# An audio tower in one kernel: the setup joined to the first loop, with its arrays laid elsewhere and the scale of the first convolution made in four parts

## The reference

```python
# 1: first convolution, 9 taps, 64 -> 128 channels, 248 outputs a sequence
sq = sum(x * x, -1); wsq = windows of 9 of sq
wnorm = sqrt(max(wsq, 0))
scale = where(wnorm < 1, 1, 1 / (wnorm + 1e-7))      # one number a token
v = conv(x, kernel) * scale
h = relu(tanh(|v| * LAM) * sign(v) + bias)
# 2: state space layer on layernorm(h): projection to 644 columns,
#    4-tap convolution, silu, scan with decays (4 heads), gate, norm, projection
h = h + mamba2(layernorm(h))
# 3: 16 experts, 2 for each token, a shared layer, and a feed-forward layer
h = h + moe_and_ffn(layernorm(h))
```

## Time and profile before

| | |
|---|---|
| median of 3 runs | 1109.79 us (1109.08 to 1115.85) |
| the profiled execution | span 1108.8 us, time 1110.55 us |
| TensorE busy | 919.5 us (83%) |
| VectorE busy | 720.5 us (65%) |
| GpSimd busy | 588.3 us (53%) |
| ScalarE busy | 495.7 us (45%) |

### The profile page before, as it was taken

The page is one execution under the profiler, slowest core; times in us unless marked ns, Lnnn a source line. Parts: engine busy times, 40 slices in busy tenths (PEclk is TensorE's granted clock), DMA queues, the critical chain, the costliest instruction groups (busy, mean ns, idle before and its releaser), DMA issues. The chain is left out here.

```text
span 1108.8 us, 22495 instructions
## 1 busy us (share of the span) xinstructions
PE 919.5 (83%) x6227; PEld 769.8 (69%) x6228; DVE 720.5 (65%) x2073; ACT 495.7 (45%) x1212; POOL 588.3 (53%) x627
## 2 busy tenths in 40 slices
PE   0488999999999999999964049999999999398887
PEld 0367777778777777878753049999999989266665
DVE  4246887787888888788874225555555545488884
ACT  3243544544544454454423025555555545144443
POOL 3133554676777767667647505555555545233342
PEclk9889999999999999998986569999999999699999
DMA  6400000000000100000084112122222221223331
GB/s 134 104 10 10 10 11 11 29 20 29 16 24 29 30 26 22 20 15 15 19 253 144 52 51 68 54 59 63 60 62 67 62 58 48 74 56 92 92 91 37
DMA packets 72012, 58.97 MB, mean 53 GB/s; under 512 B 19136, under 2 KB 61435, under 8 KB 71952
## 3 DMA queue, kind: packets, MB, share of 16 engines
q1 hardware_dynamic: 63408, 41.88, 14.7%
q0 software_dynamic: 8544, 16.34, 4.5%
HBM read 35.62 MB, written 23.81 MB: 54 GB/s over the span
## 5 line engine op out<-in xcount | busy, mean ns | idle before, releaser
L1478 POOL DMA_INDIRECT y_tokens<-arena x139 | 157.3, 1132 | 162.1 <-DVE arena L1501 116.6
L1465 ACT ACTIVATE arena<-psum,arena 128x128 f32<-128x128 f32 x556 | 158.7, 369 | 135.0 <-PE psum L1439 125.2
L1439 PE MATMUL psum<-arena 128*128 128x128 f32 x1112 | 155.8, 284 | 7.3 <-issue 3.4
L1439 PEld LDWEIGHTS psum<-arena 128*128 128x128 f32 x1112 | 136.3, 193 | 19.6 <-issue 10.8
L1452 PE MATMUL psum<-arena 128*128 x1112 | 147.4, 275 | 0.4 <-ACT arena L1465 0.4
L1098 POOL DMA_INDIRECT x_slots<-arena,idx x128 | 127.5, 996 | 34.5 <-issue 34.5
L1493 DVE COPY arena<-arena 128x644 f32 x139 | 69.2, 498 | 110.4 <-issue 56.7
L1452 PEld LDWEIGHTS psum<-arena 128*128 128x128 f32 x1112 | 135.7, 192 | 0.6 <-issue 0.6
L1209 DVE TENSOR_TENSOR_SCAN arena<-psum,arena 124x496 f32<-124x496 f32 x64 | 72.6, 1175 | 18.3 <-PE psum L751 18.3
L1652 ACT ACTIVATE arena<-psum,b_f 128x496 f32<-128x496 f32 x64 | 43.1, 673 | 58.9 <-PE psum L1633 58.9
L1501 DVE TENSOR_TENSOR arena<-psum,arena 128x128 f32<-128x128 f32 x139 | 40.5, 292 | 39.3 <-PE psum L1452 18.4
(11 more groups left out here) (255 smaller groups left out, 2138.4 us busy)
## 6 DMA issues: line engine op xcount, KB each, us to landing
arena<-x_slots SPq DMA_DIRECT2D x139, 64.5 KB
arena<-y_tokens SPq DMA_DIRECT2D x16, 448.0 KB
arena<-in_x SPq DMA_DIRECT2D x16, 256.0 KB, 2.9
out_tokens<-arena SPq DMA_DIRECT2D x16, 224.0 KB
arena<-in_ew SPq DMA_DIRECT2D x1, 2304.0 KB
y_tokens<-arena POOLq DMA_INDIRECT x139
x_slots<-zero_src SPq DMA_DIRECT2D x33, 64.5 KB, 3.8
arena<-in_x SPq DMA_DIRECT2D x4, 512.0 KB, 6.8
```

Source lines behind the costliest of these rows:

```text
L1439: last = nc.tensor.matmul(psum[:, 2 + b.q % 2, k * 128:(k + 1) * 128], w1_blk[b.q % 4][:, k * 128:(k + 1) * 128], hT[b.q % 2], start=True, ...
L1465: last = nc.scalar.activation(EHT[t.q % 2][:, k * 128:(k + 1) * 128], psum[:, 2 + t.q % 2, k * 128:(k + 1) * 128], ACT.Silu, bias=w1_blk[t ...
L1478: nc.gpsimd.indirect_dma_start(out=y_tokens, out_offset=bass.IndirectOffsetOnAxis(ap=xb[t.q][:, F:F + 1].bitcast(i32), axis=0), in_=YO[t.q ...
```

## The change

1. **One block.** The setup's instructions move into the first loop's block, each into its engine's stream. The setup arrays no longer lie in the arena under the loop's arrays but in `h_all` (residual, from row block 24 on) and `moe_all` (mixture), which are first written in later steps. Offsets in the arena stay as they were.
2. **Loads in the order of use.** First unit 0, then `tokw`, the first quarter of all tokens, `w_in` and `cw` (own count `ld_proj`), the bias (`ld_bias`), the eight others of `ld_ssm`, unit 1, the other three quarters.
3. **Scale in four parts.** Part 0 is made in step 0 (its window sums stand inside `conv(0)`), part 1 in step 0 and 1, parts 2 and 3 in step 1 and 2 (`parts_at`). The root is now a power on GpSimd (`wnorm_of`). `tanh(a)` waits for its quarter.
4. **Activation table.** A one-element Silu is the first activation; the Sqrt on ScalarE is gone.
5. **Orders in the loop, for all steps.** VectorE: the short scans of the first half come after `x_rest` (`long_scans`, `short_scans`); `hn_rest` comes after `sum_squares` and the second part of `choose`. TensorE: `output(c)` comes before `hn_transposes(a)`, and the row sums (now `row_sums`) behind it.

```diff
@@ SP
                 load(0)
+                kw = tok_kernel.rearrange("k c f -> c k f")
+                sp.dma_start(tokw[0:64, 0:5, :], kw[:, 0:TAPS:2, :]).then_inc(ld_tok, 16)
+                sp.dma_start(tokw[64:128, 0:4, :], kw[:, 1:TAPS:2, :]).then_inc(ld_tok, 16)
+                all_tokens(0)
+                sp.dma_start(w_in, in_proj).then_inc(ld_proj, 16)
+                sp.dma_start(cw, rows(conv_w, 128)).then_inc(ld_proj, 16)
+                sp.dma_start(tokb[:, :], rows(tok_bias, CH)).then_inc(ld_bias, 16)
...
                 load(1)
+                for n in range(1, XPARTS):
+                    all_tokens(n)
@@
+        def part_of(n):
+            return slice(n * NCH // XPARTS, (n + 1) * NCH // XPARTS)
+        def parts_at(t):
+            return {0: [1], 1: [2, 3]}.get(t, [])
@@ TensorE
+                def windows(n):
+                    pe.wait_ge(row_squares_ready, n + 1)
+                    if n == 0:
+                        pe.wait_ge(bands_ready, 1)
+                    k = SEQS // XPARTS
+                    sqv = sq.rearrange("p (b j) -> p j b", j=2)[:, :, n * k:(n + 1) * k]
+                    for c in range(2):
+                        for j in range(2):
+                            last = nc.tensor.matmul(psum[0:CH, 7, 2 * n * k + c * k:2 * n * k + (c + 1) * k],
+                                                    band[:, 2 * j + c, :], sqv[:, j, :],
+                                                    start=(j == 0), stop=(j == 1))
+                    last.then_inc(windows_ready, 1)
...
                     for k in range(5):
+                        if a == 0 and k == 3:
+                            windows(0)
...
                     if a is not None: conv_rows(a)
+                    for n in parts_at(t): windows(n)
...
                     if d is not None: shared_down(d, a, b)
+                    if c is not None: output(c)
                     if a is not None: hn_transposes(a, d, t)
-                    if c is not None: output(c)
+                    if c is not None: row_sums(c)
@@ ScalarE
+                act.wait_ge(warm, 1)
+                nc.scalar.activation(warm_out[:, :], warm_in[:, :], ACT.Silu)
...
+                    if t == 0:
+                        act.wait_ge(tokw_padded, 1)
+                        act.wait_ge(ld_tok, 32)
+                        high_part(0)
...
                     if a is not None: x_copy(a)
+                    if t == 0:
+                        squares(0)
+                        act.wait_ge(ld_proj, 32)
+                        high_part(1)
+                        act.wait_ge(folded, 1)
+                        high_part(2)
...
                     if a is not None: tanh(a); relu(a)
+                    for n in parts_at(t): squares(n)
@@ GpSimd
+                def wnorm_of(n):
+                    pool.wait_ge(wsq_ready, n + 1)
+                    nc.gpsimd.tensor_tensor(wnorm[:, part_of(n)], wsq[:, part_of(n)],
+                                            half[0:CH, :].to_broadcast([CH, NCH // XPARTS]), ALU.pow)\
+                        .then_inc(wnorm_ready, 1)
+                wnorm_of(0)
+                pool.wait_ge(ld_ssm, 16 * 8)
...
                     if a is not None: rstd_of(a)
+                    for n in parts_at(t): wnorm_of(n)
@@ VectorE
+                low_part(0)
+                x_rest(0)
+                row_squares(0)
+                dve.wait_ge(ld_proj, 32)
+                cwv = cw.rearrange("p (c k) -> p k c", k=KC)
+                for k in range(KC):
+                    last = V.tensor_tensor(w_tap[:, k, :], w_in[:, DI:DI + 256], cwv[:, k, 0:256], ALU.mult)
+                last.then_inc(folded, 1)
+                window_squares(0)
+                low_part(1)
+                low_part(2)
+                scale_of(0)
...
-                    if c is not None: scans(c, 0)
+                    if c is not None: long_scans(c, 0)
                     if b is not None: dt_first(b)
-                    if a is not None: x_rest(a)
-                    if c is not None: decayed_scores(c, 0)
+                    if a: x_rest(a)
+                    if c is not None: short_scans(c, 0); decayed_scores(c, 0)
...
                     if a is not None: stats(a)
+                    for n in parts_at(t): row_squares(n); window_squares(n)
+                    for n in parts_at(t - 1): scale_of(n)
...
                     if d is not None: shared_out(d)
-                    if a is not None: hn_rest(a)
                     if c is not None: sum_squares(c)
                     for n in chosen(t): choose(n, ("second",))
+                    if a is not None: hn_rest(a)
                     if c is not None: mean_squares(c); residual(c)
```

More of the change, by code:

```diff
@@ L214, in take, with rows_for, part @@
             return v
+        def rows_for(home, first):
+            at = [first]
+            def part(parts, *shape):
+                n = 1
+                for k in shape:
+                    n *= k
+                v = home[0:parts, at[0]:at[0] + n]
+                at[0] += n
+                assert at[0] <= 8192, at[0]
+                if len(shape) == 2:
+                    v = v.rearrange("p (a b) -> p a b", b=shape[1])
+                return v
+            return part
         def take_pair(name, shape):
@@ L371, in audio_tower @@
         ld_tok = sem("ld_tok")
+        ld_bias = sem("ld_bias")
+        ld_proj = sem("ld_proj")
         ld_ssm = sem("ld_ssm")
@@ L1029, in _ @@
             def _(pool):
+                nc.gpsimd.memset(ident[:, :], 0.0)
+                nc.gpsimd.memset(half[:, :], 0.5)
+                link(pool, pool_step, nc.gpsimd.memset(band, 1.0))
+                nc.gpsimd.affine_select(out=ident[:, :], in_=ident[:, :], compare_op=ALU.not_equal, fill=1.0, base=0,
+                                        pattern=[[-1, 128]], channel_multiplier=1).then_inc(ident_ready, 1)
+                for j in range(2):
+                    for c in range(2):
+                        v = band[:, 2 * j + c, :]
+                        last = nc.gpsimd.affine_select(out=v, in_=v, compare_op=ALU.is_ge, fill=0.0,
+                                                       base=128 * j - CH * c, pattern=[[-1, CH]],
+                                                       channel_multiplier=1)
@@ new lines, in _ @@
+                link(pool, pool_step, last)
+                for j in range(2):
+                    for c in range(2):
+                        v = band[:, 2 * j + c, :]
+                        last = nc.gpsimd.affine_select(out=v, in_=v, compare_op=ALU.is_ge, fill=0.0,
+                                                       base=TAPS - 1 - 128 * j + CH * c,
+                                                       pattern=[[1, CH]], channel_multiplier=-1)
+                last.then_inc(bands_ready, 1)
@@ L1030, in _ @@
+                for j in range(3, -1, -1):
+                    last = nc.gpsimd.tensor_scalar(a_neg[:, j, :], a_neg[:, 0, :], -1.0, 0.0,
+                                                   ALU.mult, ALU.add)
+                link(pool, pool_step, last)
+                pool.wait_ge(ld_bias, 16)
                 last_slot = pool.to_reg(SLOTS - 1)
```

297 lines of the change are left out of this document (138 added, 159 removed).

## The result

| | median of all runs | runs | ratio, 95% interval |
|---|---|---|---|
| before | 1112.65 us (1109.08 to 1117.64) | 20 | |
| changed | 1108.81 us (1095.97 to 1115.65) | 20 | 0.9926 [0.9904, 0.9948] |
| the same once more, on another chip (e14 below) | 1101.16 us against 1108.83 | 11 and 16 | 0.9918 [0.9886, 0.995] |

The change is worth 0.7 to 0.8%, some 8 to 9 us, where 22.5 were forecast. The changed kernel also spreads over 20 us, the one before over 9. The first trace of it comes from the slowest of its 20 runs, 1115.65 us, which the ratio leaves out as slow, with three others that are over 1.5% above the fastest. The second comes from a run of 1093.02, near the fast end of e14. I show both, since they frame the kernel; neither is its median. The first `mean_squares` belongs to step 2, the last to step 17.

The account below looks back on a forecast made before the run. In the first loop's long middle TensorE's chain was taken as the bound (busy 442.88 of 480 us). Start 13.5 plus steps 9 gave 22.5 off 1109.79: 1087.3, called 1087; own range 1078 to 1098, over the cases 1070 to 1103.

Parts of the forecast that it names:

- the clock: Steps 3 to 15: splitting TensorE's long gap into 0.6 and 1.3 ends four half-clock stretches, gaining 6 us.
- the 0 for what lies behind the steady steps: Stages after the loop start from its end, their loads too, and move with it: 0 us.
- Step 0: Joined setup and first step: `stats(0)` starts at 23.0 us instead of 44.75, 21.7 earlier.
- the rival with the port in turn: Step 0: `low_part(1)`, GpSimd's power and `low_part(2)` run in a row; scale 2.0 us later, 1089 us; chance 0.08.
- Step 1 gives back: Step 1: window sums ahead of `projection(0,1)` on TensorE make `hn_transposes(1)` later, 8.8 us lost.
- Step 2: Step 2: `conv_rows(2)` gains 2.4 us from the clock; two scales before `skip_add(0,1)` cost 1.8 at `mean_squares(0)`.
- Start in all: Setup and steps 0 to 2 together: 13.5 us earlier, bounds 10 and 18.
- The short scans: Steps 3 to 15: moving them behind `x_rest` gains 0; TensorE waits 1.3 us more for cT at `conv_rows`.
- Row sums and `hn_rest`: Steps 3 to 15: the row sums' 0.4 us wait goes and `mean_squares` comes sooner in some steps; sum 3 us.
- another length there was named as a sign of being wrong: Stages after the loop: the forecast called itself wrong if they took another length.
- the 3 and the 6 of the sum: Steps 3 to 15: 3 us from row sums and `hn_rest`, 6 from the clock; sum 9, bounds 0 and 12.
- The slower rival: Clock drops behind the moved wait before `conv_rows` in each of 13 steps, costing 22 us: 1115 us; chance 0.06.

Follow-up runs that it names:

- e14: The changed kernel run once more unaltered, for a second trace, on another chip: ratio 0.9918 to the kernel before, 1101.16 us.
- e9: The changed kernel with 12 unused TensorE products before the wait for cT (at `conv_rows`), none before `xT_lo`: ratio 0.9858 to the kernel before.
- e10: The changed kernel with 6 unused TensorE products before the wait for cT (at `conv_rows`), none before `xT_lo`: ratio 0.9858 to the kernel before.
- e3: The changed kernel with 5 unused TensorE products before the wait for `xT_lo` and 12 before that for cT: ratio 0.9857 to the kernel before.
- e6: The changed kernel with step 1's window sums behind `projection(b,3)` and both row squares made before VectorE takes them: ratio 0.9902 to the kernel before.
- e5: The changed kernel with only the four short scans put back before `x_rest`: ratio 0.9871 to the kernel before.
- e4: The changed kernel with `convT_copy` and `hhT_copy` first on ScalarE, then tanh, `bc_silu`, relu: ratio 0.9656 to the kernel before, 1076.68 us.
- e13: The changed kernel, loop's old orders, 12 unused products before the wait for `xT_lo` and 4 before the row sums: ratio 0.9854 to the kernel before.
- e8: e4 and e6 together, with the four clears of `x_st` before `low_part(0)`: ratio 0.9592 to the kernel before, 1064.33 us.
- e11: The changed kernel with the loop's old orders and 12 unused products before the wait for `xT_lo`: ratio 0.9934 to the kernel before.
- e1: The changed kernel with the loop's orders put back as before, keeping the joined setup and four-part scale: ratio 0.9871 to the kernel before.

## Why the prediction was wrong in size, point by point

The direction came out, and so did the mechanisms of the start and of the moved wait. Two terms failed: the clock, and the 0 for what lies behind the steady steps. 22.5 us were forecast and about 8 came, outside the range. Of the missing 14, e9, e10 and e3 win back 7 to 8 (0.9858 against 0.9926) by filling one wait; the rest is open. The kernel before took 1112.65 over 20 runs where the forecast started from 1109.79, the median of three; this is no part of the 22.5.

- **Step 0: right, 1 us short.** Forecast: fold from 11.2, tanh from 18.2, statistics at 23.0; measured 11.86, 19.24 and 24.0. The power on GpSimd took 3.37 beside VectorE's two-input operations and 2.89 in step 0's second part, where none ran that reads both inputs from SBUF. `low_part(1)` and `(2)` took 0.84 and 1.22, their usual length; the first still ran when the power began, the second lay wholly within it. So the rival with the port in turn falls here: GpSimd took 0.5 longer and VectorE no longer. The Trainium skill (SBUF — State Buffer, "SBUF: two separate sides") has one of the two fully blocked; this trace does not agree.
- **Step 1 gives back: right.** Forecast 8.8 of 21.7; measured 9.4 of 20.75. e6 shows that the place of the windows is its cause, and also that mending it brings little, which the prediction hadn't seen.
- **Step 2: right.** Forecast -2.4 and +1.8, measured -3.6 and +2.5. Start in all: 13.5 forecast, 12.5 and 13.6 measured at the first `mean_squares`, 11.6 and 14.9 at `x_rest(3)`.
- **The short scans: right.** No gain, the wait moved before `conv_rows`, 1.4 where 1.3 was forecast; e5 shows the first half of it, e4 the second.
- **Row sums and `hn_rest`: right in the steps.** 3 forecast, 4 by e13 against e9 in the 12 steps, but no difference in the ratio of the whole kernel.
- **The clock: wrong, in sign.** "With the gap split into 0.6 and 1.3 I expect them gone" was the failing step. It judged a gap by its length alone, by gaps that all stood in front of the convolution. The same 1.4 in front of `conv_rows`, with the mix before and transposes, scores and decays behind, called up half clock, and twice as long. Half clock cost the 12 steps 5.0 in the kernel before (389.0 against the 384.1 of e13), and 17.3 and 6.4 in the two traces of the changed one (against the 380.0 of e9). So what was to give 6 took 1 to 12 more. It wasn't length alone even before: the stretch at 498.6 us followed a wait of 0.45.
- **What lies behind the steady steps: 0 forecast, not so.** "The stages after the loop start from its end, their loads too, and move with it: 0" was the second failing step, and another length there was named as a sign of being wrong. With the wait filled (e9) the 12 steps take 9.0 less than before, the 3 and the 6 of the sum, and `x_rest(15)` comes 23.5 earlier. Yet the ratio of e9 is worth some 16. Behind `x_rest(15)` the first trace is 8.4 longer than the kernel before, the second 0.1 shorter, e3 6.8 longer, e8 0.6 shorter. The prediction had no term for the steps 15 to 17 and took the rest as fixed. Part of it changes from run to run (e5 and e6, e13 and e14); the cause stays open.
- **The slower rival** had the mechanism and the place right: half clock behind the wait before `conv_rows`, all on the path. It gave 1.7 a time and 13 times, 22 in all; it was 3.4 or more a time, in two to six of the steps 3 to 15. At 0.06 it was far too cheap, and the range should have reached to it from the forecast.

## What to carry to other kernels

When an edit moves a wait instead of removing it, look at what work the engine does on both sides of the new place, not only at the length. Here an idle piece of 0.4 us before the row sums, or of 1.4 before `conv_rows`, was followed by 6.8 us or more of half clock in some steps, and one trace was not enough to price this: compare many runs and their mean clocks. Compare all stretches of the traces too, also those that the edit leaves alone. A reorder of one engine is worth its wait only when the next engine's fixed order lets it through: here one more move on ScalarE turned 0.7% into 3.4%.

## What the runs showed of the hardware that I had not expected

- Filling an idle piece of TensorE with products whose result nobody reads made the kernel 0.7% faster (e9 against the changed kernel), by the clock alone: 0.0 us lost in 12 steps, not 7 to 19.
- The wait for the row sums was 0.36 to 0.43 us; filling it took 20.5 us of lost clock to 0.0 (e11 and e13).
- In one program on one chip, the runs fell into two groups 7 to 15 us apart, at different mean clocks (e14).
- A GpSimd power ran beside VectorE operations with two SBUF inputs and took 3.37 us, not 2.89; the VectorE operations took their usual time.

Why a stretch of half clock comes in some steps and not in their like is open, as is why the joined setup with the old orders (e1) had more of it than the kernel before (20.2 against 9.5 us lost in one trace each).
